# Gathers of a graph layer on GpSimd: the small memset behind each gather is no longer waited for before the next one

## The reference, cut to what matters

```python
pri = -jnp.arange(N, dtype=jnp.float32)
scores = jnp.where(mask, pri, neg_inf)
vals, idx = jax.lax.top_k(scores, S)                 # S = 25
feats = jax.vmap(lambda x, i: x[i])(X, idx)          # the gather
agg = jnp.where(valid[..., None], feats, neg_inf).max(axis=2)
h = jnp.concatenate([X, agg], axis=-1)
x = _layernorm(x + relu(h @ W + b))                  # layer 0
...
attention = softmax(where(adj == 0, NEG, leaky_relu(e_src + e_dst)))
x = _layernorm(x + _layernorm_heads(relu(attention @ h + bias) + h))   # layer 1
```

## Time and profile before

| | us |
|---|---|
| median of 3 runs | 5598.53 (5595.39 to 5600.58) |
| profiled execution | 5598.51 |
| its span in the trace | 5596.7 |
| POOL busy | 3855.2 (69%), 3200 gathers and 3200 memsets |
| DVE busy | 3947.8 (71%) |
| PE busy | 3722.0 (67%) |
| ACT busy | 2181.3 (39%) |

### The profile page before, as it was taken

One profiled execution on the slowest core, in us unless ns is written; L12 is line 12 of the kernel. 1 busy time (PEld: TensorE's weight loads), 2 busy tenths in 40 slices (PEclk: granted clock), 3 DMA queues, 4 the chain that ended last, 5 costly groups with the idle time before them and its releaser, 6 DMA issues.

```text
span 5596.7 us, 60889 instructions
## 1 busy us (share of the span) xinstructions
PE 3722.0 (67%) x12546; PEld 1650.0 (29%) x12546; DVE 3947.8 (71%) x12445; ACT 2181.3 (39%) x4674; POOL 3855.2 (69%) x6404
## 2 busy tenths in 40 slices
PE   2232267667676767777777777677777766777787
PEld 1111133323323333333333233323323332333232
DVE  4444477777777777777777777777777777777666
ACT  3333334334444434444443444444344443433212
POOL 5777777777777777777777777777777777777300
PEclk8555577777777777767777777777777777777888
DMA  3333334434334443443444444344444443443100
GB/s 123 116 114 121 114 123 125 131 124 128 123 120 128 130 128 124 128 126 119 129 125 130 125 127 124 122 127 131 128 123 128 125 133 115 133 124 110 54 23 27
DMA packets 264414, 658.87 MB, mean 118 GB/s; under 512 B 62161, under 2 KB 128978, under 8 KB 247762
## 3 DMA queue, kind: packets, MB, share of 16 engines
q0 software_dynamic: 153600, 419.64, 25.9%
q1 hardware_dynamic: 110546, 236.66, 12.1%
HBM read 605.73 MB, written 50.33 MB: 117 GB/s over the span
## 4 chain that ended last, share of the span: by engine, by line
POOL 59%; issue 22%; PE 9%; DVE 7%; ACT 1%; DMA 1%; POOLq 1%; SPq 0%; DVEq 0%; another core or an unknown queue 0%; ACTq 0%
POOL rows L495 53%; POOL idle L498 6%; PE acc L1258 6%; DVE uv L837 2%; DVE rmax L856 1%; DMA rows<-in_x_dram,idx 1%; PE pB L1226 1%; PE rq L1196 1%; PE acc L1184 1%; DVE top L724 1%; ACT raw L574 0%; PE pA L1213 0%; DVE key_b L726 0%; PE pB L1227 0%; POOLq L491 0%
## 5 line engine op out<-in xcount | busy, mean ns | idle before, releaser
L495 POOL DMA_INDIRECT rows<-in_x_dram,idx x3200 | 3469.2, 1084 | 1380.8 <-POOL idle L498 971.4
L1258 PE MATMUL acc<-uv,hs 128*65 128x512 f32 x4096 | 2195.1, 693 | 79.2 <-ACT raw L574 58.8
L837 DVE SCALAR_TENSOR_TENSOR uv<-rq,qinv,maskT 128x512 f32<-128x512 f32 x2048 | 1502.9, 740 | 614.6 <-PE acc L1258 281.4
L1258 PEld LDWEIGHTS acc<-uv,hs 128*65 128x65 f32 x4096 | 629.0, 161 | 1357.2 <-issue 1316.4
L856 DVE TENSOR_TENSOR rmax<-rmax,rows 128x1280 f32<-128x1280 f32 x384 | 570.7, 1486 | 530.6 <-DMA rows<-in_x_dram,idx 530.3
L1236 PE MATMUL pA<-id,xh 128*128 128x128 f32 x256 | 87.4, 444 | 920.7 <-DVE xh L819 906.9
L648 ACT ACTIVATE x1T<-pA 128x256 f32<-128x256 f32 x128 | 49.1, 383 | 1239.3 <-PE pA L1236 1239.3
L639 ACT ACTIVATE xaT<-pA 128x512 f32<-128x512 f32 x128 | 76.4, 597 | 1049.8 <-PE pA L1213 916.3
L1226 PE MATMUL pB<-w_sb,xaT 128*128 128x256 f32 x1024 | 363.2, 517 | 113.5 <-DVE pad L739 67.7
L498 POOL MEMSET idle<- 128x8 f32 x3200 | 385.8, 121 | 2.6
L1236 PEld LDWEIGHTS pA<-id,xh 128*128 128x128 f32 x256 | 36.7, 202 | 1023.3 <-DVE xh L819 1006.9
(11 more groups left out here) (117 smaller groups left out, 4699.4 us busy)
## 6 DMA issues: line engine op xcount, KB each, us to landing
adj_sb<-in_adj_dram SPq DMA_DIRECT2D x128, 1024.0 KB
rows<-in_x_dram,idx POOLq DMA_INDIRECT x3200
xh_dram<-xh SPq DMA_DIRECT2D x128, 256.0 KB
xr<-xh_dram SPq DMA_DIRECT2D x64, 512.0 KB
xt<-in_x_dram SPq DMA_DIRECT2D x128, 128.0 KB
out_dram<-xr SPq DMA_DIRECT2D x32, 512.0 KB
w_sb<-in_L_gnn_W_dram SPq DMA_DIRECT2D x1, 512.0 KB
wcat<-in_L_gnn_W_dram SPq DMA_DIRECT2D x2, 128.0 KB
```

What stands on the lines that cost most here:

```text
L495: nc.gpsimd.indirect_dma_start(rows[:, c, r * C:(r + 1) * C], None, x_rows, bass.IndirectOffsetOnAxis(ap=idx[u][:, k:k + 1], axis=0)).then ...
L837: stt = nc.vector.scalar_tensor_tensor(uv[k][:, i, :], rq[i][:], inv, m, ALU.max, ALU.mult)
L1258: last = nc.tensor.matmul(acc[i][0:HW, :], hs[:, (1 - quad.par) * JT + jt, h, :], uv[k][:, i, :], start=(jt == 0), stop=(jt == JT - 1))
```

## The change

`idle` becomes a tile of 2 x 25 bytes for each partition, with a byte of its own for each parity of the tile and each gather. The memset still stands behind each gather, writes that one byte, and adds one to a semaphore of its parity, but GpSimd doesn't wait for it there. It waits once, ahead of a tile, for the 25 memsets of the tile two before, whose bytes are about to be written again. No other instruction moves; the clearing of the semaphore at the end of each tile is gone. `p` is the parity of the tile, `quad.reach` gives the count to wait for, and none where it is zero.

```diff
-        idle = sb("idle", [P, 8], F32)
+        idle = sb("idle", [P, 2, S], U8)
...
-        s_pace = sem("s_pace")
+        s_pace = [sem(f"s_pace{p}") for p in range(2)]
...
                 for v in quad.reach(lambda q: QT * q + u + 1):
                     pool.wait_ge(s_idx, v)
-                pace = Chain(pool, s_pace)
+                p = u % 2
+
+                for v in quad.reach(lambda q: S * (2 * q + u // 2)):
+                    pool.wait_ge(s_pace[p], v)
                 for c in range(CH):
...
                             bass.IndirectOffsetOnAxis(ap=idx[u][:, k:k + 1], axis=0)).then_inc(s_rows[c], 16)
-                        pace.then(nc.gpsimd.memset(idle[:], 0.0))
-                pace.end()
+                        nc.gpsimd.memset(idle[:, p, k:k + 1], 0).then_inc(s_pace[p], 1)
```

## The result

The changed kernel took **6610.03 us** (median of 4 runs, 6590.65 to 6616.37) against 5596.96 us of the kernel before (4 runs, 5587.47 to 5600.58): ratio 1.1807, 95% interval 1.1778 to 1.1837. It was slower, not faster. The experiments make that sentence longer: **on two chips (2 and 6) it is 9% faster than before, on chip 5 and on the one of this result, whose number is not on record, 18 to 19% slower, with the same code.** On a further chip (1) the unedited change was not run; close variants of it were 16 to 17% slower there. I call the second kind *stalling chips* and the first kind *plain chips*.

A forecast was written before the change was run, and what follows sets the result against it. POOL, pacing itself by waiting behind its own memsets, was taken to bound the first stage, with the middle stage mixed with DVE and PE: 5598.5 - 150 - 200 = 5248.5, say 5250 us, range 5035 to 5410.

The forecast's parts named there:

- POOL runs ahead until the five buffers are full, and DVE and PE set the pace: Middle stage: at 31 us a tile POOL fills the buffers, so the gain is at most DVE's waits for rows, 361.6 us.
- The paragraph on DMA: DMA engines have room: gathers take 25.9% of their time, 0.40 in the middle stage, about 0.5 later in the first.
- The pause of 0.27 us goes, beat 1.07 us: POOL between gathers: an unwaited instruction needs no pause, so the beat falls from 1.34 to 1.07 us.
- (b): Rival: GpSimd needs 0.27 us between memset and gather anyhow; about 5590 us if nothing goes; chance 0.06.
- The chunk's preparation (0.62 us): POOL at chunk starts: 0.89 - 0.27 us, four per tile, taken to vanish; if it stays, 33.5 us a tile instead of 31.
- First stage, -150 us, end near 540: First 16 tiles, POOL the bound: 162.8 us of pauses less 13 of added hold-ups; bounds 100 and 200.
- Middle stage, -200 us, tile 38.8 us: 112 tiles: 161.8 us of PE's waits for `agg`, 32.6 of chunk 1, a little for chunk 2; bounds 100 and 361.6.
- of the waits for chunks 3 and 4 only what PE waited for `agg` comes back: Middle stage: of DVE's waits for rows ahead of chunks 3 and 4, only 161.8 us are gained, as PE is late next.
- PE might catch up: Upper bound of the middle stage, 361.6 us gained: denser work may lift PE's granted clock, 0.75 there.
- POOL then waits for `rmax`: Middle stage sign: POOL, ahead with buffers full, waits for `rmax` in place of its waits behind the memset.
- (a): Rival: DVE's two-SBUF-operand instructions wait for gathers, 6.8 us a tile, 760 us less the 350 won, 6010 us; chance 0.08.
- (c): Rival: middle stage gives the time back as waits for `rq`, `acc` and `xh`'s followers, gaining some 50 us; 5400 us; chance 0.11.

The follow-up runs named there:

- f1: The changed kernel itself, nothing edited, run on chip 2 against the kernel before: 5109.80 us, ratio 0.9118.
- e3: The changed kernel without the memsets and without the waits ahead of a tile, on chip 1: 6496.78 us, ratio 1.1583 against the kernel before.
- e8: The changed kernel gathering 128 of the 256 numbers of each row, other half left out, on chip 6: 5096.27 us, ratio 0.9087 against the kernel before.
- e5 to e8: The changed kernel on chip 6 with, per gather, two memsets (5204.56 us), two sequencer increments (5108.33) or three (5104.18) instead of one memset, or half rows (5096.27).

## Why the prediction was wrong, point by point

**Where the sign came from.** The forecast was 5250 us, faster. The result's chip gave 6610. The step that failed is "POOL runs ahead until the five buffers are full, and DVE and PE set the pace": it takes for granted, and puts at nothing without a reason, what a denser beat of POOL does to the hand-overs between the other engines. The two terms that are added up on that footing, -150 us in the first stage and -200 in the middle one, measured -8 and +1012 us. The paragraph on DMA looked for a limit at the DMA engines' busy share, and there was none: a gather's last packet ends 1.5 to 2.4 us behind the instruction before and 1.5 to 2.0 after (means by place in the tile). What broke was the passing on of PE's semaphore updates while dense gathers ran, on chips of one kind: 650 of 1927 late, against 225 of 1798 before. The rows that I had read don't show it, but the trace did, in the "remote" line quoted above; I had looked at the chain, where it rounds to 0%. The forecast weighed one chip's trace, and the difference between chips is larger than any of its terms.

**The terms, on plain chips.** f1 lets the rest be checked, span 5111.3 us:

```profile
45.00:579.00 534.00, 176.91 (x904) 112.62 (x901) 313.75 (x1111) 215.96 (x404) 459.00 (x799) 0.58 0.46 143
579.00:4750.00 4171.00, 3146.51 (x10849) 1422.75 (x10850) 3356.54 (x10693) 1863.14 (x4016) 3306.31 (x5597) 0.77 0.44 136
4750.00:5111.00 361.00, 291.49 (x730) 105.17 (x730) 238.16 (x570) 77.72 (x236) 2.47 (x6) 0.85 0.08 26
```

- *The pause of 0.27 us goes, beat 1.07 us*: wrong in size. 0.19 us stays, the beat is 1.25. The evidence of the earlier trace rows was on memsets behind gathers or memsets, not on a gather behind anything, and the prediction named this gap in rival (b) and then gave it 0.06. e3 shows that the gap is the gather's: without memset it is 0.30 us, and the sum stays 1.25. The chunk's preparation (0.62 us) did go entirely: chunk starts have the same 0.19.
- *First stage, -150 us, end near 540*: it ended at 579, -111 us, inside the bounds. (The bound of 100 counts 80 chunk preparations; at the four a tile that the text names it is 64, and the bound 110.) The beat explains it: 33.4 us a tile instead of 31. 0.18 us of beat x 25 = 4.5 us a tile would be 35.5; some of the delays under DVE's maxima fell away, since a gather now takes 1030 ns there against 1080.
- *Middle stage, -200 us, tile 38.8 us*: -379 us, 37.2 us a tile, just past the upper bound of 361.6. The failed step is "of the waits for chunks 3 and 4 only what PE waited for `agg` comes back". All came back. The waits in f1, stage 579 to 4750:

```profile
DVE uv L839 <- PE rq L1198: 266.7, 56, 8.4
DVE uv L839 <- PE acc L1260: 240.8, 233, 3.8
...
PE pA L1215 <- DVE agg L870: 10.4, 2, 8.0
...
DVE rmax L858 <- DMA rows<-in_x_dram,idx: 6.5, 4, 2.4
```

  DVE's wait for rows fell from 358.4 to 6.5 us and that for PE's `rq` and `acc` rose only from 453.9 to 507.5; I had expected some 150 more. PE followed: its granted clock there was 0.77 instead of 0.75, and its matmuls of `acc` took 670 instead of 693 ns on average, 4096 x 23 ns = 94 us less work. That PE might catch up stood in the bounds with the clock as its reason; I took the middle and should have leaned to that end.
- *POOL then waits for `rmax`*: right, 346.5 us there (14.4 before).
- *The sum*: 5598.5 - 111 - 379 + 4 (last stage, 361 against 357) = 5112, measured 5113 for f1's profiled execution (span 5111.3). Two errors in opposite directions and a third of the gain from where I did not expect it.

**The rivals.** (a), slower, was the only one of that sign, at 6010 us: its mechanism did not occur. DVE's folds took 691/691/693 ns after too, its maxima over `rmax` and `rows` 1483 to 1489 ns on average in every trace, and DVE's waits in the stalled trace are for PE, not for POOL. The evidence that the prediction gave against it was weaker than it sounds: the maximum of the earlier trace rows began only 0.13 us before the gather's end (400.64 and 399.82 + 0.95), not "well before". What it had right was the place where harm could come from, GpSimd's freed 0.27 us. The rule of the Trainium skill that stood beside it ("SBUF — State Buffer", "Who interferes with whom") doesn't speak of semaphore updates, and by its own half the trace still disagrees: by these averages a DVE instruction that starts inside a gather isn't held. (b), the pause isn't the wait's: true for 0.19 of the 0.27 us, yet the time still fell on plain chips, because of the 0.62 us at chunk starts and the 0.08 of each beat: (0.08 x 25 + 0.62 x 4) = 4.5 us of POOL's tile, enough to take POOL off the chain. (c), the middle stage gives it back: false on plain chips. On stalling ones it gives back 1012 us, by another mechanism.

**What would show it.** The list asked for the pause, the beat, the end of the first stage and waits for `rmax`. The waits for `rmax` came on both kinds of chip, the rest in part; none of its lines asked whether the hand-overs stay on time. "remote" as a releaser in a one-core trace (43.1 us before, for one line), and a share for an unknown queue in the chain (0% in the earlier trace rows), is the line that was missing.

## What stays open

- What in a dense run of gathers delays the updates on the stalling chips: their bytes, the number of their descriptors, or what GpSimd writes for them. e8 would have told, had it met such a chip. Why the chips differ is open too.
- The records of the stalling chips lack 5 to 11% of PE's updates, four memsets included, where nothing stalls; those of plain chips are complete to within 1%. The kernel before's trace lacks 13% and has 225 late ones, where none of the twelve traces of plain chips has one, so it very probably comes from a chip of the stalling kind. Whether the incomplete record is a second effect of the same cause, or whether recording has a part in the stall, wasn't tried: every run here was recorded.
- Two chips of the plain kind were seen, and of the stalling kind chips 1 and 5 and that of the result, which may be one of these. The kernel before left no trace on a plain chip. How common each is can't be said from that.
- No version beat the kernel before on both kinds. On plain chips the changed kernel (5106 to 5110 us) is as fast as any that computes everything (5104 to 5108); on stalling chips the kernel before is the fastest, and its spacing of 1.58 us is close to what such a chip bears (225 late updates, none of them costly as far as its time shows).

## What to carry to other kernels

Removing a pause on GpSimd's indirect gathers raises the density of gathers for everyone, so price it by what the other engines' semaphore updates do, and look in the trace for late updates, "remote" releasers and bursts before looking at engines. A POOL that paces itself leaves slack that may be doing work: keep a pace that can be set. And where a result is off by more than any term of its sum, run the unedited kernel again on another chip before editing it: e5 to e8 seemed to cure what was a difference between chips.

## What the runs showed that was not expected

- An indirect gather of 128 rows of 1 KB costs GpSimd 1.25 us each, back to back: 0.95 in the record and 0.30 before the next can start, with nothing, a 0.12 us memset, or two or three sequencer increments between. With half the bytes it is 1.25 as well (e8). The least is thus not set by the bytes.
- Two or three semaphore increments of GpSimd's sequencer behind each gather cost nothing, since the sequencer works ahead (5104 to 5108 us, as without).
- On chips 1 and 5 and that of the result a third of PE's semaphore updates came over 0.25 us late while gathers ran 1.25 us apart, half of them by more than 11 us and the longest by 29 to 38, many of them together 2 to 4 us behind the last gather; on chips 2 and 6 none did, at the same beat. Already at a spacing of 1.58 us one in eight was late, by up to 4.6 us. The ratio of the same change was 1.1866 on one chip and 0.9111 on another, with runs of each within 0.4%.
